# Causal mask copied into PSUM by ScalarE, a written-out table of PSUM banks, and one reciprocal moved, in a causal attention + gated feed-forward kernel

## The chip, the cores and the metric

One core of a Trainium2 chip runs the whole program once. The metric is device time in microseconds (us), the median over separate executions. Nothing is shared with other cores.

## The reference

Four sequences of 1024 tokens with 128 features go through one transformer layer with post-norm: causal attention with 8 heads of 128 and rotary positions, a residual and a layer norm, then a gated feed-forward part of width 512 with four layers, a residual and a layer norm. Cut to what matters here (all fp32):

```python
q, k, v = (jnp.einsum('btm,mhd->bthd', x, w) for w in (w_aq, w_ak, w_av))   # (4, 1024, 8, 128)
q, k = _rope(q), _rope(k)
s = jnp.einsum('bihd,bjhd->bhij', q, k) / 128
mask = (i < j)[None, None, :, :]                 # i query, j key
s = s - 1e30 * mask
p = jax.nn.softmax(s, axis=-1)
r = jnp.einsum('bhij,bjhd,hdm->bim', p, v, w_ao)
x = layernorm(x + r); x = layernorm(x + ffn(x))
```

## The kernel before

The work is 32 heads in all (8 of each of 4 sequences), one after the other, and then the feed-forward part, which the change doesn't touch. A head has 1024 queries in 8 blocks of 128, numbered `ib` 0 to 7. Block `ib` needs the keys of blocks 0 to `ib`, so its row of scores is (`ib` + 1) x 128 columns wide.

Every product that must keep fp32 accuracy is made of three fp32r matmuls (high x high, high x low, low x high), so whatever TensorE produces in PSUM is later split: ScalarE copies the high part out, VectorE subtracts it and writes the low part. One block goes through these operations:

- TensorE: `scores`. Three matmuls for each half of the row (one half up to 512 columns, two equal halves above), and one more, `ident_r` x `mask_r`, which adds -1e30 above the diagonal of the last 128 columns (L407 to L411).
- VectorE: `negative_max` (L678).
- ScalarE: `exponentiate` (L557), which writes `probs` and the row sum.
- VectorE: `inverse_sum` (L684), a reciprocal of one column.
- GpSimd: `normalize` (L802), which multiplies `probs` by it.
- TensorE: `transpose_probs` (L420), one or two fills of a PSUM bank.
- ScalarE: `transposed_high` (L569), and VectorE: `transposed_low` (L694), which write `pT`.
- TensorE: `attend` (L330 with `pT,vals`), in pieces.

The order is written out by hand as eight steps of each head, `s` = 0 to 7, and each engine runs its own part of a step in order, held only by semaphores. In step `s` TensorE issues the scores of block `s + 2` and the transposes of block `s`; VectorE issues the reciprocal of block `s + 1`, the maximum of block `s + 2` and the low halves of block `s`; ScalarE the exponential of block `s + 1` and the high halves of block `s`; GpSimd normalizes block `s + 1`. So blocks 0 and 1 of the next head already start in steps 6 and 7. Between these lies the projection of the next head's queries and keys, in four tiles of 512 columns: TensorE makes tiles 0 and 1 in step 0 and tiles 2 and 3 in step 2 (`QK_STEP`), VectorE multiplies each by sine and cosine (`rope_products`, L706 and L708), a transfer swaps halves, GpSimd adds (L813), ScalarE and GpSimd split (L579, L819). Heads go in pairs, `off` 0 and 1, here called the even and the odd head. The values for both are projected in steps 4 to 7 of the even one only (`V_STEP`, L586 on ScalarE, L726 on VectorE). A Fori loop runs over the pairs of one sequence.

PSUM has 8 banks of 512 columns. Bank 7 holds the output of `attend`. Scores of even blocks use banks 0 and 1, of odd blocks banks 2 and 3, and rows up to 512 wide leave banks 1 and 3 free for a while. Transposes (`t`), projected tiles (`qk`) and values (`v`) use banks 4, 5 and 6, and banks 1 and 3 in the steps `LEND1` and `LEND3`. `plan_banks` gives each use the bank that was used longest ago. TensorE waits, before each use, for the last reader of the bank's previous use (`wait_for_banks`): VectorE's low half for a `t` or `v`, the cosine product for a `qk` tile, the exponential for scores.

Of the kernel before, what the change touches and what calls it, by code (L numbers as in the profile page):

```python
# [27 lines left out]
P = 128  # L28
# [31 lines left out]
LEND1 = (6, 7, 0)  # L60
LEND3 = (1, 2)
FILLS_OF = [1 if i < 4 else 2 for i in range(NI)]
FIRST_FILL = [sum(FILLS_OF[:i]) for i in range(NI)]
NT = sum(FILLS_OF)
NQK, NV = len(QK_STEP), len(V_STEP)
PV_BANK = 7


def plan_banks():

    uses = {}
    last = dict.fromkeys(range(PV_BANK), 0)

    for off in range(2):
        for s in range(NI):
            ib, tile_off = (s + 2) % NI, off + (s + 2) // NI
            first = 2 * (ib % 2)
            lent = [bank for bank, free in ((1, LEND1), (3, LEND3)) if s in free]  # L80

            after = ([("t", off, FIRST_FILL[s] + k) for k in range(FILLS_OF[s])]
                     + [("qk", off + 1, j) for j in range(NQK) if QK_STEP[j] == s]
                     + [("v", 0, c) for c in range(NV) if V_STEP[c] == NI * off + s])
            for use in [("s", tile_off, ib)] + after:
                if use[0] == "s":
                    uses[use] = [first, first + 1] if ib >= 4 else [first]
                else:
                    uses[use] = [min([4, 5, 6] + lent, key=lambda b: last[b])]
                for bank in uses[use]:  # L90
                    last[bank] = len(uses)
    return uses
# [23 lines left out]
def run(nc, outer, sem, rT, ident, qk_split, v_split, xT, w_q, w_k, w_vT, w_o, rope_in, ident_in, mask_in,  # L116
# [7 lines left out]
    ident_r = sb("ident_r", [P, P], F32R, outer)  # L124
    mask_r = sb("mask_r", [P, P], F32R, outer)
# [15 lines left out]
    mask_f = sb("mask_f", [P, P], F32, pre)  # L141
# [17 lines left out]
    score_ps = psum[:, :4 * BANK].rearrange("p (s h c) -> p s h c", s=2, h=2)  # L159
# [18 lines left out]
    masks_ready = sem("masks_ready")  # L178
    W_SAVED = 16 * (len(weight_parts) + 2)


    scores_ready = (sem("scores_ready"), NI)
# [24 lines left out]
    def score_halves(ib):  # L207

        width = (ib + 1) * P
        return (1, width) if width <= BANK else (2, width // 2)  # L210
# [115 lines left out]
    def split_products(out_ap, left, right, first, last):  # L326

        terms = ((0, 0), (0, 1), (1, 0))
        for i, (a, b) in enumerate(terms):
            ins = nc.tensor.matmul(out_ap, left[a], right[b], start=first and i == 0, stop=last and i == 2)  # L330
        return ins

    with nc.Block() as block:
        @block.sync
        def _(sp):
# [5 lines left out]
            sp.dma_start(mask_f[:], mask_in).then_inc(masks_loaded, 16)  # L341
# [52 lines left out]
        def _(pe):  # L394
            def scores(head, ib):

                wait_for(pe, rope_low, head, 1 if ib < 4 else 3)

                pair, off = head if ("s", head[1], ib) in USES else (head[0] - 1, head[1] + 2)
                wait_for_banks(pe, pair, "s", off, ib)  # L400
                q, k = ([qk[:, parity(head), which, part] for part in range(2)] for which in range(2))
                halves, half = score_halves(ib)
                for h in range(halves):
                    dst = score_ps[:, ib % 2, h, :half]
                    left = [a[:, ib * P:(ib + 1) * P] for a in q]
                    right = [a[:, h * half:(h + 1) * half] for a in k]
                    nc.tensor.matmul(dst, left[0], right[0], start=True, stop=False)  # L407
                    if h == halves - 1:
                        nc.tensor.matmul(dst[:, half - P:], ident_r[:], mask_r[:], start=False, stop=False)
                    nc.tensor.matmul(dst, left[0], right[1], start=False, stop=False)  # L410
                    last = nc.tensor.matmul(dst, left[1], right[0], start=False, stop=True)  # L411
                last.then_inc(scores_ready[0], 1)

            def transpose_probs(head, ib):
                wait_for(pe, probs_ready, head, ib)
                for f in range(FILLS_OF[ib]):
                    nth = FIRST_FILL[ib] + f
                    wait_for_banks(pe, head[0], "t", head[1], nth)
                    for jb in range(4 * f, min(4 * f + 4, ib + 1)):
                        last = nc.tensor.transpose(bank("t", head[1], nth)[:, (jb % 4) * P:(jb % 4 + 1) * P],  # L420
                                                   probs[:, ib % 4, jb * P:(jb + 1) * P], ident[:])
                    last.then_inc(t_filled[0], 1)
# [49 lines left out]
            def step(head, s, b):  # L472
# [7 lines left out]
                if before_first(head) and s == NI - 2:  # L480
                    pe.wait_ge(masks_ready, 1)
# [27 lines left out]
        def _(act):  # L509
# [39 lines left out]
            def exponentiate(head, ib):  # L549

                n = parity(head) * NI + ib
                wait_for(act, max_ready, head, ib)
                old_head, old = earlier(head, ib, 4, NI)
                wait_for(act, t_filled, old_head, FIRST_FILL[old] + FILLS_OF[old] - 1)
                width = (ib + 1) * P
                halves, half = score_halves(ib)
                nc.scalar.activation(probs[:, ib % 4, :width].rearrange("p (h c) -> p h c", h=halves),  # L557
                                     score_ps[:, ib % 2, :halves, :half], ACT.Exp,
                                     bias=neg_max[:, n:n + 1], accum_out=row_sum[:, n:n + 1]).then_inc(exp_done[0], 1)

# [28 lines left out]
            def step(head, s, b):  # L589
# [3 lines left out]
                if before_first(head) and s == 1:  # L593
                    act.wait_ge(masks_loaded, 32)
                    nc.scalar.activation(ident_r[:], ident[:], ACT.Copy)
                    nc.scalar.activation(mask_r[:], mask_f[:], ACT.Copy).then_inc(masks_ready, 1)
                if before_first(head) and s == 2:
                    high_of_weights(1)
                if before_first(head) and s == 4:
                    act.wait_ge(vo_ready, 1)  # L600
# [28 lines left out]
        def _(dve):  # L629
# [44 lines left out]
            def negative_max(head, ib):  # L674
                n = parity(head) * NI + ib
                wait_for(dve, scores_ready, head, ib)
                halves, half = score_halves(ib)
                nc.vector.tensor_reduce(neg_max[:, n:n + 1], score_ps[:, ib % 2, :halves, :half], AX.XY, ALU.max,  # L678
# [65 lines left out]
            def step(head, s, b):  # L744
# [5 lines left out]
                if exists(step_on(head, (s + 1) // NI)):  # L750
# [26 lines left out]
                for target, j in rope_tasks(head, s, QK_STEP):  # L777
                    rope_products(target, j)
                if before_first(head) and s == 2:
# [14 lines left out]
        def _(pool):  # L794
            nc.gpsimd.memset(warm[:], 0.0).then_inc(warm_zero, 1)
# [605 lines left out]
```

## Time and profile before

| | |
|---|---|
| median of 3 executions | 1031.66 us (1029.73 to 1032.62) |
| the profiled execution: its time | 1031.09 us |
| its span, first to last instruction | 1029.2 us |
| TensorE, share of the span busy | 96% |
| VectorE | 79% |
| ScalarE | 58% |
| GpSimd | 53% |
| mean granted TensorE clock | 0.991 of full |

The span is 1.9 us shorter than the time. Attention fills it to about 760 us, the feed-forward part the rest. The busy shares are means over both parts, and a TensorE matmul counts as busy to its modelled end, which lies past the start of the next one, so short waits of TensorE do not show as idle. Two consecutive heads take about 46 us.

### The profile page before, as it was taken

The numbers are of one execution on the slowest core, as the hardware profiler recorded it, in microseconds if no ns is written. First come the engines' busy times: TensorE is split into PE (matmuls) and PEld (weight loads), VectorE is DVE, ScalarE is ACT, GpSimd is POOL, SyncE is SP. The second block draws the span as 40 slices with busy tenths as digits, with TensorE's granted clock in tenths as the row PEclk, the third lists the DMA queues.
The fourth block names the chain that finished last, engine by engine and source line by source line (L and its number), as shares of the span: only waits on it lengthen the run. The fifth ranks groups of instructions, "written<-read, shape, count | busy, mean of one in ns | idle before, by whom it ended". The sixth has DMA issues, their size and how long they took to land.

```text
span 1029.2 us, 19670 instructions
## 1 busy us (share of the span) xinstructions
PE 985.7 (96%) x5648; PEld 856.6 (83%) x5648; DVE 816.9 (79%) x1789; ACT 593.6 (58%) x1270; POOL 543.4 (53%) x549
## 2 busy tenths in 40 slices
PE   4899999999999999999999999999989999999995
PEld 3788898888888898888888888888878888888884
DVE  5788888888888888888888888888866778586744
ACT  3566666676656666666666666665665252433521
POOL 3666767678666767877666767766772101000000
PEclk9999999999999999999999999999999999999998
DMA  6723232222222322222235322222400000000000
GB/s 198 245 53 76 58 77 66 61 52 62 63 66 67 69 74 51 63 52 62 63 70 178 78 62 53 62 53 64 119 1 1 1 1 21 1 20 0 1 20 21
DMA packets 33979, 61.96 MB, mean 60 GB/s; under 512 B 5504, under 2 KB 7296, under 8 KB 33536
## 3 DMA queue, kind: packets, MB, share of 16 engines
q1 hardware_dynamic: 30816, 55.21, 21.5%
q10 hardware_dynamic: 3104, 6.03, 1.7%
q8 instruction: 29, 0.48, 0.2%
q14 instruction: 30, 0.25, 0.1%
HBM read 22.16 MB, written 5.24 MB: 27 GB/s over the span
## 4 chain that ended last, share of the span: by engine, by line
PE 71%; DVE 11%; issue 7%; ACT 4%; POOL 3%; DVEq 1%; ACTq 0%; POOLq 0%
PE psum L330 24%; PE psum L1047 17%; PE psum L420 9%; PE psum L410 5%; PE psum L407 5%; PE psum L1020 4%; PE psum L411 4%; DVE neg_max L678 3%; POOL probs L802 2%; DVE pT L694 2%; PE psum L1062 2%; ACT probs L557 2%; ACT pT L569 2%; DVE by_sin L706 2%; DVE by_cos L708 1%
## 5 line engine op out<-in xcount | busy, mean ns | idle before, releaser
L802 POOL TENSOR_SCALAR probs<-probs,inv_sum 128x128 f32<-128x128 f32 (+7 forms) x256 | 191.3, 747 | 222.0 <-DVE inv_sum L684 221.5
L569 ACT ACTIVATE pT<-psum 128x512 fp32r<-128x512 f32 (+3 forms) x384 | 174.2, 490 | 132.3 <-PE psum L420 130.3
L330 PE MATMUL psum<-pT,vals 128*128 128x512 f32 (+3 forms) x1152 | 243.0, 351 | 1.0 <-DVE pT L694 1.0
L557 ACT ACTIVATE probs<-psum,neg_max 128x128 f32<-128x128 f32 (+7 forms) x256 | 190.3, 743 | 85.9 <-DVE neg_max L678 80.8
L694 DVE TENSOR_TENSOR pT<-psum,pT 128x512 fp32r<-128x512 f32 (+3 forms) x384 | 201.0, 551 | 33.4 <-ACT pT L569 29.5
L678 DVE TENSOR_REDUCE neg_max<-psum 128x1 f32<-128x128 f32 (+7 forms) x256 | 191.7, 749 | 27.0 <-PE psum L411 26.1
L330 PEld LDWEIGHTS psum<-pT,vals 128*128 128x128 f32 x1152 | 188.7, 190 | 23.5 <-DVE pT L694 1.2
L420 PE MATMUL psum<-ident,probs 128*128 128x128 f32 x1152 | 173.0, 277 | 10.7 <-POOL probs L802 8.2
L1047 PE MATMUL psum<-hid,w 128*128 128x512 f32 x768 | 176.3, 390 | 0.0
L813 POOL TENSOR_TENSOR swapped<-by_cos,swapped 128x512 f32<-128x512 f32 x127 | 163.0, 1294 | 18.4 <-DMA swapped<-by_sin 17.5
L1047 PEld LDWEIGHTS psum<-hid,w 128*128 128x128 f32 x768 | 143.7, 188 | 29.5
L420 PEld LDWEIGHTS psum<-ident,probs 128*128 128x128 f32 x1152 | 134.8, 141 | 36.1 <-issue 8.6
L819 POOL TENSOR_TENSOR qk<-swapped,qk 128x512 fp32r<-128x512 f32 x126 | 162.6, 1290 | 0.0
L407 PE MATMUL psum<-qk 128*128 128x384 f32 (+5 forms) x384 | 137.7, 359 | 9.4 <-DVE qk L721 3.7
L410 PE MATMUL psum<-qk 128*128 128x384 f32 (+5 forms) x384 | 143.0, 372 | 0.0
L411 PE MATMUL psum<-qk 128*128 128x384 f32 (+5 forms) x384 | 131.6, 343 | 0.0
L330 PE MATMUL psum<-x_moving,w_stage 128*128 128x512 f32 (+1 forms) x384 | 108.1, 419 | 11.2 <-DVEq L650 8.8
L579 ACT ACTIVATE qk<-swapped 128x512 fp32r<-128x512 f32 x128 | 80.7, 631 | 41.8 <-POOL swapped L813 39.8
L1147 ACT ACTIVATE value<-psum,scales 128x512 f32<-128x512 f32 x64 | 43.0, 689 | 93.0 <-PE psum L1047 93.0
L330 PEld LDWEIGHTS psum<-x_moving,w_stage 128*128 128x128 f32 x384 | 69.7, 195 | 26.6 <-DVEq L650 8.8
L407 PEld LDWEIGHTS psum<-qk 128*128 128x128 f32 x384 | 72.8, 190 | 21.5 <-issue 10.1
L706 DVE TENSOR_TENSOR by_sin<-psum,rope 128x512 f32<-128x512 f32 x128 | 87.2, 681 | 2.5 <-DMA rope<-rope_in 2.5
(87 smaller groups left out, 1132.6 us busy)
## 6 DMA issues: line engine op xcount, KB each, us to landing
swapped<-by_sin SPq DMA_DIRECT2D x256, 128.0 KB, 2.3
w_stage<-qk_split SPq DMA_DIRECT2D x30, 256.0 KB, 2.7
wv_stage<-v_split SPq DMA_DIRECT2D x15, 256.0 KB, 2.6
ffn_raw<-g SPq DMA_DIRECT2D x2, 1024.0 KB, 7.8
out<-y SPq DMA_DIRECT2D x8, 256.0 KB, 2.0
qk_split<-rT ACTq DMA_DIRECT2D x1, 1536.0 KB, 7.7
ffn_raw<-xT SPq DMA_DIRECT2D x3, 512.0 KB, 7.8
y<-x_tok SPq DMA_DIRECT2D x1, 1536.0 KB, 8.5
```

Of the source, the lines that this page charges most:

```text
L330: ins = nc.tensor.matmul(out_ap, left[a], right[b], start=first and i == 0, stop=last and i == 2)
L407: nc.tensor.matmul(dst, left[0], right[0], start=True, stop=False)
L410: nc.tensor.matmul(dst, left[0], right[1], start=False, stop=False)
L411: last = nc.tensor.matmul(dst, left[1], right[0], start=False, stop=True)
L420: last = nc.tensor.transpose(bank("t", head[1], nth)[:, (jb % 4) * P:(jb % 4 + 1) * P], probs[:, ib % 4, jb * P:(jb + 1) * P], ident[:])
L557: nc.scalar.activation(probs[:, ib % 4, :width].rearrange("p (h c) -> p h c", h=halves), score_ps[:, ib % 2, :halves, :half], ACT.Exp, bia ...
L569: nc.scalar.activation(pT[chunk][:, 0, 4 * f:4 * f + n_blocks, (ib % 4) * P:(ib % 4 + 1) * P], bank("t", head[1], nth)[:, :n_blocks * P].r ...
L678: nc.vector.tensor_reduce(neg_max[:, n:n + 1], score_ps[:, ib % 2, :halves, :half], AX.XY, ALU.max, negate=True).then_inc(max_ready[0], 1)
L694: nc.vector.tensor_tensor(low, bank("t", head[1], nth)[:, :n_blocks * P].rearrange("p (j i) -> p j i", i=P), high.bitcast(F32), ALU.subtra ...
L802: nc.gpsimd.tensor_scalar(p, p, inv_sum[:, n:n + 1], 1.0, ALU.mult, ALU.mult).then_inc(probs_ready[0], 1)
L813: nc.gpsimd.tensor_tensor(swapped[:, j], by_cos[:, j], swapped[:, j], ALU.add).then_inc(rope_done[0], 1)
L1047: last = nc.tensor.matmul(ps[:, c, o], self.w_at(base, a, k * HID, o * P), hid[:, c, layer, b, k], start=k == 0 and i == 0, stop=k == HT - ...
```

## The change

Three edits.

1. The mask. The identity matmul goes away. A tile `mask` of 512 columns in SBUF holds zeros and, in the last 128, the triangle of -1e30. ScalarE copies as many of its last columns as needed into PSUM ahead of the scores (`write_mask`), and the three score matmuls of that piece then accumulate onto it. A row above 512 columns is now cut so that the piece with the diagonal (`near`: 256, 256, 384 and 512 columns for blocks 4 to 7) lies in the first of the two banks and the older keys in the second; the row is contiguous across both, with the key blocks rotated, and `prob_block` takes this back at the transposes. The total of columns is the same as before. ScalarE issues the mask of block `s + 3` in step `s`, right after the exponential of block `s + 1`, and waits for that exponential, which reads the same bank. TensorE issues the older keys first, then waits for the mask. At the start GpSimd writes the zeros and TensorE runs one matmul of 512 columns into banks 0 and 2.
2. The banks of `t`, `qk` and `v` come from a table over the pair of heads.
3. VectorE takes the reciprocal of block 2 in step 0, between the products of rotation tiles 0 and 1, where it stood at the start of step 1.

```diff
+MASK_COLS = BANK
+def score_layout(ib):
+    width = (ib + 1) * P
+    return width, width if ib < 4 else max(2 * P, width - BANK)
+FILL_BANKS = ((4, 6, 3, 5, 5, 6, 5, 6, 1, 5, 3, 4), (6, 3, 4, 4, 6, 4, 5, 6, 4, 1, 6, 3))
+QK_BANKS = ((1, 5, 5, 4), (5, 4, 5, 6))
+V_BANKS = (4, 4, 6, 1)
...
+    def score_row(ib):
+        width, near = score_layout(ib)
+        first = BANK - near if ib >= 4 else 0
+        return score_ps[:, ib % 2, first:first + width]
+    def masked_piece(ib):
+        return score_row(ib)[:, :score_layout(ib)[1]]
...
-                halves, half = score_halves(ib)
-                for h in range(halves):
-                    dst = score_ps[:, ib % 2, h, :half]
-                    left = [a[:, ib * P:(ib + 1) * P] for a in q]
-                    right = [a[:, h * half:(h + 1) * half] for a in k]
-                    nc.tensor.matmul(dst, left[0], right[0], start=True, stop=False)
-                    if h == halves - 1:
-                        nc.tensor.matmul(dst[:, half - P:], ident_r[:], mask_r[:], start=False, stop=False)
-                    nc.tensor.matmul(dst, left[0], right[1], start=False, stop=False)
-                    last = nc.tensor.matmul(dst, left[1], right[0], start=False, stop=True)
+                left = [a[:, ib * P:(ib + 1) * P] for a in q]
+                width, near = score_layout(ib)
+                if width > near:
+                    split_products(score_row(ib)[:, near:], left, [a[:, :width - near] for a in k], True, True)
+                wait_for(pe, mask_written, head, ib)
+                last = split_products(masked_piece(ib), left, [a[:, width - near:width] for a in k], False, True,
+                                      onto_mask=True)
...
+            def write_mask(head, ib):
+                wait_for(act, exp_done, *earlier(head, ib, 2, NI))
+                near = score_layout(ib)[1]
+                nc.scalar.activation(masked_piece(ib), mask[:, MASK_COLS - near:], ACT.Copy).then_inc(mask_written[0], 1)
...
                 if exists(ahead):
                     exponentiate(ahead, (s + 1) % NI)
+                if exists(step_on(head, (s + 3) // NI)):
+                    write_mask(step_on(head, (s + 3) // NI), (s + 3) % NI)
...
-                if exists(step_on(head, (s + 1) // NI)):
+                if exists(step_on(head, (s + 1) // NI)) and s != 1:
                     inverse_sum(step_on(head, (s + 1) // NI), (s + 1) % NI)
...
                 for target, j in rope_tasks(head, s, QK_STEP):
+                    if s == 0 and j == 1 and exists(head):
+                        inverse_sum(head, 2)
                     rope_products(target, j)
```

On ScalarE, step 5 of the first (even) head: exponential, rotated tile, two high halves of the transposed block, values. Before:

```order
L557 ACTIVATE probs,row_sum<-psum,neg_max 128x896 [waits t_filled,max_ready]
L579 ACTIVATE qk<-swapped 128x512 [waits rope_done]
L569 ACTIVATE pT<-psum 128x4x128 [waits t_filled]
L569 ACTIVATE pT<-psum 128x2x128 [waits t_filled]
L586 ACTIVATE vals<-psum 128x512 [waits v_projected]
L557 ACTIVATE probs,row_sum<-psum,neg_max 128x1024 [waits t_filled,max_ready]
L579 ACTIVATE qk<-swapped 128x512 [waits rope_done]
```

The same step with the change (line numbers are those of the changed kernel):

```order
L573 ACTIVATE probs,row_sum<-psum,neg_max 128x896 [waits t_filled,max_ready]
L580 ACTIVATE psum<-mask 128x128 [waits exp_done]
L600 ACTIVATE qk<-swapped 128x512 [waits rope_done]
L590 ACTIVATE pT<-psum 128x4x128 [waits t_filled]
L590 ACTIVATE pT<-psum 128x2x128 [waits t_filled]
L607 ACTIVATE vals<-psum 128x512 [waits v_projected]
L573 ACTIVATE probs,row_sum<-psum,neg_max 128x1024 [waits t_filled,max_ready]
L580 ACTIVATE psum<-mask 128x256 [waits exp_done]
```

A copy into PSUM now stands behind every exponential, and everything else of the step moves down behind it.

On VectorE, step 0 of the same head and the beginning of step 1: products of tiles 0 and 1, then the reciprocal and the maximum. Before:

```order
L706 TENSOR_TENSOR by_sin<-psum,rope 128x512 [waits rope_low,swap_done0,qk_projected]
L708 TENSOR_TENSOR by_cos<-psum,rope 128x512
L706 TENSOR_TENSOR by_sin<-psum,rope 128x512 [waits rope_low,swap_done1,qk_projected]
L708 TENSOR_TENSOR by_cos<-psum,rope 128x512
L661 TENSOR_TENSOR rT<-raw_w,rT 128x6x128 [waits qk_w_high]
L684 RECIPROCAL inv_sum<-row_sum 128x1 [waits exp_done]
L678 TENSOR_REDUCE neg_max<-psum 128x1 [waits scores_ready]
```

With the change:

```order
L728 TENSOR_TENSOR by_sin<-psum,rope 128x512 [waits rope_low,swap_done0,qk_projected]
L730 TENSOR_TENSOR by_cos<-psum,rope 128x512
L706 RECIPROCAL inv_sum<-row_sum 128x1 [waits exp_done]
L728 TENSOR_TENSOR by_sin<-psum,rope 128x512 [waits rope_low,swap_done1,qk_projected]
L730 TENSOR_TENSOR by_cos<-psum,rope 128x512
L684 TENSOR_TENSOR rT<-raw_w,rT 128x6x128 [waits qk_w_high]
L700 TENSOR_REDUCE neg_max<-psum 128x1 [waits scores_ready]
```

The reciprocal moves ahead of two products, which now stand behind its wait for the exponential. (The row on `rT` is a single one of the first head.)

On TensorE, the scores of block 6, before:

```order
L407 MATMUL psum<-qk 128x448 [waits exp_done,rope_low]
L410 MATMUL psum<-qk 128x448
L411 MATMUL psum<-qk 128x448
L407 MATMUL psum<-qk 128x448
L409 MATMUL psum<-mask_r,ident_r 128x128
L410 MATMUL psum<-qk 128x448
L411 MATMUL psum<-qk 128x448
```

With the change:

```order
L346 MATMUL psum<-qk 128x512 [waits exp_done,rope_low]
L346 MATMUL psum<-qk 128x512 x2
L346 MATMUL psum<-qk 128x384 [waits mask_written]
L346 MATMUL psum<-qk 128x384 x2
```

One matmul is gone, and the second piece has a wait of its own.

## Rows read from the trace of the kernel before

**Rows 1.** The page's part 1: busy time of each engine, share, instructions.

```profile
PE 985.7 (96%) x5648; PEld 856.6 (83%) x5648; DVE 816.9 (79%) x1789; ACT 593.6 (58%) x1270; POOL 543.4 (53%) x549
```

**Rows 2.** Windows: start:end, length, busy us (instructions) by engine, PEclk, DMA share, GB/s.

```profile
454.30:466.60 12.30, 12.30 (x89) 11.44 (x88) 10.96 (x23) 10.44 (x25) 9.05 (x9) 1.00 0.10 28
478.40:488.60 10.20, 9.84 (x65) 8.54 (x64) 8.40 (x18) 8.15 (x20) 8.97 (x9) 1.00 0.00 0
466.60:478.40 11.80, 11.68 (x66) 10.04 (x65) 10.01 (x21) 5.54 (x13) 7.00 (x8) 1.00 0.50 114
```

**Rows 3.** Timeline of TensorE, block 7's scores, even head: start, us, instruction.

```profile
455.56 0.40 PE L407 MATMUL psum<-qk 128*128 128x512 f32 x1
...
456.26 0.39 PE L407 MATMUL psum<-qk 128*128 128x512 f32 x1
...
457.06 0.82 PE L420 MATMUL psum<-ident,probs 128*128 128x128 f32 x6
```

**Rows 4.** Groups by shape, ScalarE's copies: busy us, mean ns, idle before.

```profile
L569 ACT ACTIVATE pT<-psum 128x512 fp32r<-128x512 f32 x192 | 111.0, 596 | 84.3 <-PE psum L420 82.6
L579 ACT ACTIVATE qk<-swapped 128x512 fp32r<-128x512 f32 x128 | 80.7, 631 | 41.8 <-POOL swapped L813 39.8 <-DVE swapped L715 0.2
...
L569 ACT ACTIVATE pT<-psum 128x384 fp32r<-128x384 f32 x64 | 31.5, 492 | 5.9 <-PE psum L420 5.5
...
L569 ACT ACTIVATE pT<-psum 128x256 fp32r<-128x256 f32 x64 | 24.8, 387 | 34.8 <-PE psum L420 34.8
...
L569 ACT ACTIVATE pT<-psum 128x128 fp32r<-128x128 f32 x64 | 17.7, 276 | 7.4 <-PE psum L420 7.3
```

**Rows 5.** Timeline of ScalarE, steps 4 to 7 of an even head.

```profile
454.94 0.77 ACT L569 ACTIVATE pT<-psum 128x512 fp32r<-128x512 f32 x2 [2.13 <-PE psum L420]
...
457.15 0.20 ACT L557 ACTIVATION_READ_ACCUMULATOR probs<-psum,neg_max 128x1 f32 x1
457.24 0.63 ACT L579 ACTIVATE qk<-swapped 128x512 fp32r<-128x512 f32 x1
...
459.11 1.11 ACT L557 ACTIVATE probs<-psum,neg_max 128x1024 f32<-128x1024 f32 x1
...
462.83 1.09 ACT L569 ACTIVATE pT<-psum 128x512 fp32r<-128x512 f32 x2 [0.29 <-PE psum L420]
```

**Rows 6.** The chain that ended last, even into odd head: start, us, what.

```profile
464.06 0.68 DVE pT L694
...
468.67 0.61 DVE by_cos L708
469.28 0.04 issue
469.32 0.41 PE psum L407
```

**Rows 7.** Timeline of TensorE: block 2's transposes of that odd head.

```profile
470.42 0.49 PE L420 MATMUL psum<-ident,probs 128*128 128x128 f32 x3
```

**Rows 8.** The chain that ended last, steps 5 to 7 of the odd head.

```profile
480.91 1.24 DVE neg_max L678
...
483.81 1.11 POOL probs L802
484.91 0.12 issue
485.03 0.67 PE psum L420 x4
```

**Rows 9.** Timeline of ScalarE, odd into even head.

```profile
485.72 1.09 ACT L569 ACTIVATE pT<-psum 128x512 fp32r<-128x512 f32 x2 [0.39 <-PE psum L420]
486.69 0.48 ACT L557 ACTIVATE probs<-psum,neg_max 128x256 f32<-128x256 f32 x1
```

**Rows 10.** Timeline of TensorE: block 3's scores of the next head.

```profile
488.60 0.40 PE L407 MATMUL psum<-qk 128*128 128x512 f32 x1
```

**Rows 11.** The chain that ended last, steps 0 to 2 of an even head.

```profile
444.08 0.68 DVE by_sin L706
...
445.36 0.07 DVE inv_sum L684
```

**Rows 12.** Timeline of GpSimd, the same place: block 2 normalized.

```profile
445.63 0.59 POOL L802 TENSOR_SCALAR probs<-probs,inv_sum 128x384 f32<-128x384 f32 x1 [3.23 <-DVE inv_sum L684]
```

**Rows 13.** Timeline of TensorE, the same place: block 2 transposed.

```profile
446.35 0.43 PE L420 MATMUL psum<-ident,probs 128*128 128x128 f32 x2 [0.19 <-DVE pT L694]
```

More of the change, by code:

```diff
@@ L79, in plan_banks @@
             first = 2 * (ib % 2)
[L80 to L91, printed above, removed]
+            uses["s", tile_off, ib] = [first, first + 1] if ib >= 4 else [first]
+            for nth in range(FIRST_FILL[s], FIRST_FILL[s] + FILLS_OF[s]):
+                uses["t", off, nth] = [FILL_BANKS[off][nth]]
+            for j in range(NQK):
+                if QK_STEP[j] == s:
+                    uses["qk", off + 1, j] = [QK_BANKS[off][j]]
+            for c in range(NV):
+                if V_STEP[c] == NI * off + s:
+                    uses["v", 0, c] = [V_BANKS[c]]
     return uses
@@ L122, in sb @@
         return where.enter_context(nc.sbuf_tensor(name, shape, dt))
[L124 to L125 removed]
+    mask = sb("mask", [P, MASK_COLS], F32, outer)
     ffn = FeedForward(nc, outer, sem, rT, ident, ffn_raw, ffn_loaded, x_tok, scales_in, out)
@@ L324, in wait_for_banks, with split_products @@
                 break
-    def split_products(out_ap, left, right, first, last):
+    def split_products(out_ap, left, right, first, last, onto_mask=False):
         terms = ((0, 0), (0, 1), (1, 0))
         for i, (a, b) in enumerate(terms):
-            ins = nc.tensor.matmul(out_ap, left[a], right[b], start=first and i == 0, stop=last and i == 2)
+            ins = nc.tensor.matmul(out_ap, left[a], right[b], start=first and i == 0, stop=last and i == 2,
+                                   skip_group_check=onto_mask)
         return ins
@@ L479, in step @@
                     last.then_inc(vo_ready, 1)
-                if before_first(head) and s == NI - 2:
-                    pe.wait_ge(masks_ready, 1)
+                    pe.wait_ge(mask_zero, 1)
+                    pe.wait_ge(masks_loaded, 32)
+                    for masked_bank in (0, 2):
+                        nc.tensor.matmul(psum[:, masked_bank * BANK:(masked_bank + 1) * BANK], mask[:, :P], mask[:],
+                                         start=True, stop=True).then_inc(scores_opened, 1)
                 if is_first(head) and s == 1:
@@ L676, in negative_max @@
                 wait_for(dve, scores_ready, head, ib)
-                halves, half = score_halves(ib)
-                nc.vector.tensor_reduce(neg_max[:, n:n + 1], score_ps[:, ib % 2, :halves, :half], AX.XY, ALU.max,
+                nc.vector.tensor_reduce(neg_max[:, n:n + 1], score_row(ib), AX.X, ALU.max,
                                         negate=True).then_inc(max_ready[0], 1)
@@ L777, in step @@
                 for target, j in rope_tasks(head, s, QK_STEP):
+                    if s == 0 and j == 1 and exists(head):
+                        inverse_sum(head, 2)
                     rope_products(target, j)
+                if s == 0 and exists(head) and not rope_tasks(head, s, QK_STEP):
+                    inverse_sum(head, 2)
                 if before_first(head) and s == 2:
@@ L794, in _ @@
         def _(pool):
+            nc.gpsimd.memset(mask[:, :MASK_COLS - P], 0.0).then_inc(mask_zero, 1)
             nc.gpsimd.memset(warm[:], 0.0).then_inc(warm_zero, 1)
```

29 lines of the change are left out of this document (13 added, 16 removed).

## The prediction, made before the changed kernel ran

> **What bounds the kernel now.** I read the shares first. TensorE is busy 96% of the span [rows 1], which says that a removed matmul should shorten the time by its own length. But a busy matmul is counted past the start of the next, so I read the windows and then the chain that ended last through a pair of heads. ScalarE is busy 10.44 of 12.30 us in steps 4 to 7 of the even head, 8.15 of 10.20 in those of the odd one, and only 5.54 of 11.80 in between [rows 2]. It has room on average and hardly any where the even head projects the values. The chain then shows that TensorE is only one of three bounds in turn:
>
> - In steps 2 to 4 of each head TensorE itself is the chain.
> - In steps 4 to 7 of the even head it runs through ScalarE, which works from 454.94 with a single gap of 0.29 us ahead of 462.83 [rows 5]. It goes on through VectorE: low halves of block 7 at 464.06, and the cosine product of tile 1, which ends at 469.28. That product frees the bank in which the odd head's block 4 gets its scores, and TensorE starts them at 469.32 [rows 6].
> - In the odd head it goes maximum of block 7 (480.91, 1.24 us), exponential, reciprocal, normalization (483.81, 1.11 us), transposes at 485.03 [rows 8]. No TensorE work is in it for 4 us.
> - At the start of the even head it goes rotation products, reciprocal of block 2 at 445.36 [rows 11], normalization at 445.63 after GpSimd sat idle for 3.23 us [rows 12], and so to the transposes of block 2 at 446.35, ahead of which TensorE was idle 0.19 us [rows 13].
>
> **The mask matmuls removed.** Block 7 shows the same three matmuls with and without the mask. The first half takes 455.56 to 456.26, 0.70 us; the second, with it, 456.26 to 457.06, 0.80 us [rows 3]. A mask matmul costs 0.10 us of TensorE's time. There are 8 x 32 = 256 of them: 26 us if TensorE were the bound everywhere. The new cut of the rows has the same columns in all, so it costs nothing by itself.
>
> **The mask copies added.** No row shows ScalarE copying from SBUF into PSUM. The nearest rows are its copies from PSUM: 276, 387, 492 and 596 ns for 128, 256, 384 and 512 columns; from SBUF to SBUF 512 columns take 631 ns [rows 4]. I take the first set, since they have all four sizes, and 0.04 us more for the wait on its own exponential, which is what a released engine took at 469.28 [rows 6]. Without a wait the next instruction starts 0.11 us ahead of the end of the row-sum read (457.24 against 457.15 + 0.20) [rows 5]; this overlap is lost ahead of the copy and comes back behind it. So the prices are 0.32, 0.43, 0.53 and 0.64 us. Per head there are one, three, two and two of these sizes: 3.95 us. Two heads' 7.9 us of ScalarE against some 18 us idle in 46 us fit on average. Bounds for one copy: 0.1 us less (a faster write to PSUM, or the wait hidden) and 0.15 us more (the slower SBUF source, and a late wake-up).
>
> The Trainium skill (ScalarE: Activation LUTs, "Step-by-step: what each stage is for") says that ScalarE writes into PSUM faster than into SBUF. All rows 4 write into SBUF, so the trace can't say. If the rule takes 0.1 us off each copy, the sum below ends near 1009.
>
> **What each stretch of a pair gains**, taken at TensorE's own positions:
>
> (a) Step 4 of the even head to block 2's transposes of the odd one. The copy for block 7 lies in the 2.13 us in which ScalarE is idle ahead of 454.94 [rows 5] and costs nothing. Those for blocks 0, 1 and 2 stand in the full stretch: 0.32 + 0.43 + 0.53 = 1.28, less the gap of 0.29, so block 7's high halves come 1.0 us later. VectorE waits for them and is full from 464.06 on. Queued behind are values, block 2's maximum and the rotation products, all 1.0 us later, and 0.1 more for the reciprocal now ahead of tile 1: its cosine product ends at 470.4 and not at 469.28 [rows 6]. By the table, block 4's scores no longer wait for it, since bank 1 now held value tile 3; block 2's transposes do (bank 4), and they stand at 470.42 today [rows 7]. The table takes back just what the copies cost. Gain 0.
>
> (b) From there to step 4 of the odd head, TensorE bound: two masks, 0.2.
>
> (c) Odd head to block 7's transposes. Between the exponentials of blocks 6 and 7 stands the copy for block 0 (0.32), which makes ScalarE, and not the maximum, the last to be ready. The 0.2 of (b) is taken back, and 485.03 [rows 8] stays. Gain -0.2.
>
> (d) To block 2's transposes of the next even head. The copies for blocks 1 and 2 cost 0.96 less the gap of 0.39, so block 1's exponential starts at 487.3 and not at 486.69 [rows 9]; with 0.57 for itself and 0.64 for block 3's copy this ends at 488.5. Block 3's scores start at 488.60 today [rows 10]: just held. Behind them two masks (0.2) and the 0.19 us wait for the reciprocal [rows 13] go, which now comes after tile 0, some 1.2 us earlier (tile 1's products start at 444.08, the reciprocal stood at 445.36) [rows 11]. Gain 0.4.
>
> (e) To step 4 of that head: two masks, 0.2.
>
> Sum 0 + 0.2 - 0.2 + 0.4 + 0.2 = 0.6 us a pair, 16 pairs: 10 us. What the start gains and loses (two opening matmuls, a memset, while TensorE still waits) is left out. The moved bank waits around tiles 0 and 1 give perhaps 1 us more. The profiled execution took 1031.1 us with its 1.9 us outside the span; less 11 this is 1020. The median of the runs is 0.6 us above that execution, within their spread.
>
> **The rivals.**
>
> - *ScalarE's copies are hidden.* If the copies are 0.1 cheaper, or the chain gives way because the table and the early reciprocal free more than I see, TensorE sets the pace again: 26 us of masks, and 16 x 2 x 0.19 = 6 of waits for block 2, so 1000. For it: ScalarE is idle over a third of attention. Against it: the 0.29 gap [rows 5]. With only the cheaper copies, 7 of them stand on the chain of a pair (three in (a), four in (c) and (d)): 7 x 0.1 x 16 = 11 us, 1009.
> - *Slower: the copies stretch the exponential-to-transposes chain.* Each copy stands ahead of the high halves and of the next exponential. With 7 copies on the chain, 0.6 / 7 = 0.09 us more per copy takes all the gain; 0.15 more gives 7 x 0.15 x 16 = 17 us: 1037. The place is block 7's transposes in both heads. For it: there is no slack there. Against: everything measured near is copied at the price that I took.
> - *No change*: 0.05 to 0.12 us more per copy, between the two, 1028 to 1034.
> - *It doesn't do what it says*: TensorE's 0.10 us for a mask may be hidden by weight loads, so that only the waits change. Rows 3 speak against it; it would give the slower case.
>
> **The numbers.** Part of the gain returned, 1010 to 1028: 0.50. Hidden (998 to 1010): 0.25. No change: 0.12. Slower: 0.13. The likeliest gives 1020. The range of 1003 to 1032 leaves out about 2 in 10. A measurement of this kernel tells 0.3% (3 us) from no change: faster 0.76, same 0.12, slower 0.12.
>
> **What would show it.** Right: ScalarE's busy share up by some 110 us; its copies at 0.28 to 0.60 us; windows of steps 4 to 7 of the even head as long as today (12.3 us) with ScalarE nearly full; the gain in steps 0 to 4; GpSimd's 3.2 us wait ahead of block 2 down to about 2; maxima and exponentials of the same length as now. Wrong: TensorE waiting for the mask itself in many steps, exponentials of blocks 0 and 7 more than 1 us later against TensorE, or reads of rows across two banks that got longer.

## The result and the profile after

| | before | changed |
|---|---|---|
| median | 1031.25 us (1029.45 to 1032.62, 5 runs) | 1014.91 us (1014.57 to 1015.58, 5 runs) |
| the profiled execution: time, span | 1031.09 us, 1029.2 us | 1014.79 us, 1012.9 us |

The ratio is 0.9844, with a 95% interval of 0.9832 to 0.9857: 16.3 us less, where 11 were forecast. The granted clock is the same (0.990 of full, 0.991 before).

Shares of the page, part 1, which answers to [rows 1], and part 4, the chain that ended last by engine (before, the same line of the page had TensorE 71%, VectorE 11%, ScalarE 4%, GpSimd 3%):

```profile
PE 968.7 (96%) x5396; PEld 828.6 (82%) x5396; DVE 815.9 (81%) x1789; ACT 694.5 (69%) x1524; POOL 543.7 (54%) x550
PE 59%; ACT 11%; POOL 10%; DVE 9%; issue 7%; DMA 2%; DVEq 0%; ACTq 0%; POOLq 0%; SPq 0%
```

ScalarE is busy 100.9 us more (694.5 - 593.6), and it is now a larger part of the chain. TensorE is still "96% busy": the share hides the whole change.

The groups by shape: ScalarE's new copies (L580), and one group that answers to [rows 4]. Columns: busy us, mean ns of one | idle before:

```profile
L590 ACT ACTIVATE pT<-psum 128x512 fp32r<-128x512 f32 x192 | 108.9, 584 | 22.5 <-PE psum L434 22.5
...
L580 ACT ACTIVATE psum<-mask 128x512 f32<-128x512 f32 x64 | 38.5, 602 | 2.0
L580 ACT ACTIVATE psum<-mask 128x256 f32<-128x256 f32 x96 | 37.3, 388 | 3.0
L580 ACT ACTIVATE psum<-mask 128x384 f32<-128x384 f32 x64 | 31.7, 496 | 2.0
...
L580 ACT ACTIVATE psum<-mask 128x128 f32<-128x128 f32 x32 | 9.0, 282 | 1.0
```

A copy takes what one from PSUM takes, and the wait ahead of it adds 8.0 us of idle time over 256 copies, 0.03 each. ScalarE's idle time ahead of `transposed_high` of 512 columns fell from 84.3 us [rows 4] to 22.5: the copies fill it.

To see where the time came from I take the prediction's own five stretches of a pair: each begins and ends at the start of the transposes of some block, rows of L434 in TensorE's timeline. Here is one pair; `x5` are block 4's transposes, `x3` block 2's, `x8` block 7's:

```profile
445.30 0.71 PE L434 MATMUL psum<-ident,probs 128*128 128x128 f32 x5
...
461.02 0.55 PE L434 MATMUL psum<-ident,probs 128*128 128x128 f32 x3
...
468.79 0.71 PE L434 MATMUL psum<-ident,probs 128*128 128x128 f32 x5
...
475.58 1.09 PE L434 MATMUL psum<-ident,probs 128*128 128x128 f32 x8 [0.48 <-POOL probs L829]
...
482.35 0.49 PE L434 MATMUL psum<-ident,probs 128*128 128x128 f32 x3
...
490.06 0.71 PE L434 MATMUL psum<-ident,probs 128*128 128x128 f32 x5
```

The differences are (a) 15.72, (b) 7.77, (c) 6.79, (d) 6.77 and (e) 7.71 us. The same differences as means over the 12 pairs in the middle of the span, from the one traced execution of each kernel (the experiments come below):

| us | (a) | (b) | (c) | (d) | (e) | pair |
|---|---|---|---|---|---|---|
| before | 16.01 | 7.93 | 6.65 | 7.29 | 7.97 | 45.86 |
| changed | 15.81 | 7.75 | 6.78 | 6.75 | 7.75 | 44.84 |
| gain | 0.20 | 0.18 | -0.13 | 0.54 | 0.22 | 1.02 |
| forecast | 0 | 0.2 | -0.2 | 0.4 | 0.2 | 0.6 |
| mask alone | 16.73 | 7.70 | 6.78 | 7.59 | 7.75 | 46.55 |
| table alone | 15.83 | 7.97 | 6.65 | 7.29 | 7.98 | 45.73 |
| reciprocal alone | 16.08 | 7.94 | 6.65 | 6.97 | 7.94 | 45.58 |
| table and reciprocal | 15.78 | 7.94 | 6.65 | 6.75 | 7.94 | 45.06 |
| before, no mask matmuls | 15.79 | 7.75 | 6.65 | 7.29 | 7.79 | 45.27 |
| changed, no copies | 15.42 | 7.71 | 6.65 | 6.54 | 7.75 | 44.06 |
| changed, dearer copies | 16.52 | 7.75 | 7.16 | 7.23 | 7.95 | 46.61 |
| copies for 4 to 7 only | 16.02 | 7.71 | 6.65 | 6.79 | 7.70 | 44.87 |
| copies for 4 to 6 only | 15.71 | 7.71 | 6.65 | 6.66 | 7.72 | 44.45 |

16 pairs x 1.02 = 16.3 us: the pairs hold the gain. (The changed kernel begins its first pair 2.5 us later than before, and that pair is 3.4 us shorter and not 1.0; the two about cancel.)

The chain that ended last, in stretch (a) of the pair above (start, us, what), answers to [rows 5, 6]:

```profile
453.38 0.48 ACT vals L607
453.86 0.36 ACT probs L573 x2
...
454.68 0.59 ACT pT L590
...
455.90 0.68 DVE pT L716
...
460.37 0.61 DVE by_cos L730
461.02 0.55 PE psum L434 x3
```

This is what the prediction said: the chain runs through ScalarE and VectorE to tile 1's cosine product, and what waits for that is now block 2's transposes, not block 4's scores. In the 12 pairs the transposes start 0.08 us after that product ends; before it was 1.17, with block 4's scores between.

The windows of the changed kernel answer to [rows 2] (same columns; steps 4 to 7 of the even head, what follows, steps 4 to 7 of the odd one from the start of its block 4's transposes at 468.79, all cut to the same lengths as before; the second overlaps the third by 0.6 us):

```profile
445.30:457.60 12.30, 12.24 (x86) 11.05 (x85) 10.58 (x22) 11.46 (x28) 9.68 (x10) 1.00 0.13 42
457.60:469.40 11.80, 11.71 (x67) 10.13 (x66) 10.92 (x23) 7.65 (x17) 7.03 (x8) 1.00 0.49 112
468.79:478.99 10.20, 9.66 (x61) 8.06 (x60) 8.25 (x19) 9.37 (x23) 9.65 (x10) 1.00 0.05 17
```

ScalarE's busy time, the fourth of the five, is 11.46 of 12.30 us (10.44 before), 7.65 (5.54) and 9.37 of 10.20 (8.15). The copies nearly filled ScalarE in both crowded stretches.

One wait of TensorE for a mask is not in the idle notes. It stands at the end of the odd head, where block 2's scores of the next head follow block 7's transposes. First two rows of TensorE before; then, in the changed kernel, ScalarE's mask copy for block 2 and the scores that accumulate onto it:

```profile
485.03 1.09 PE L420 MATMUL psum<-ident,probs 128*128 128x128 f32 x8 [0.23 <-POOL probs L802]
485.88 0.42 PE L407 MATMUL psum<-qk 128*128 128x384 f32 x1
...
476.14 0.49 ACT L580 ACTIVATE psum<-mask 128x384 f32<-128x384 f32 x1
476.69 0.79 PE L346 MATMUL psum<-qk 128*128 128x384 f32 x3
```

Before, the scores start 0.85 us after the transposes (485.88 - 485.03). Now it is 1.11 (476.69 - 475.58), 0.06 after the copy's end at 476.63. In the 12 pairs these scores start 0.05 us after the copy's end in nine and 0.14 after it in three. The transposes count as busy to their modelled end, so this wait shows as no idle time.

### The profile page after: what moved, and what is told of

The parts are those of the page before. It is cut to its first block, busy times and chain, and to the rows that moved or that the text cites. A ratio compares the mean times of both kernels' runs of the same rounds, so it can differ in the third digit from the quotient of the medians.

```text
span 1012.9 us, 19514 instructions
## 1 busy us (share of the span) xinstructions
PE 968.7 (96%) x5396; PEld 828.6 (82%) x5396; DVE 815.9 (81%) x1789; ACT 694.5 (69%) x1524; POOL 543.7 (54%) x550
## 4 chain that ended last, share of the span: by engine, by line
PE 59%; ACT 11%; POOL 10%; DVE 9%; issue 7%; DMA 2%; DVEq 0%; ACTq 0%; POOLq 0%; SPq 0%
PE psum L346 28%; PE psum L1074 17%; PE psum L434 6%; ACT probs L573 5%; PE psum L1047 4%; ACT pT L590 4%; POOL probs L829 4%; DVE by_cos L730 3%; POOL qk L846 3%; POOL swapped L840 3%; PE psum L1089 2%; DVE by_sin L728 2%; DVE pT L716 1%; DVE neg_max L700 1%; DMA rope<-rope_in 1%
## 5 line engine op out<-in xcount | busy, mean ns | idle before, releaser
L346 PE MATMUL psum<-qk 128*128 128x512 f32 (+3 forms) x1152 | 254.7, 348 | 7.2 <-ACT psum L580 3.4
L346 PEld LDWEIGHTS psum<-qk 128*128 128x128 f32 x1152 | 195.4, 190 | 37.5 <-issue 9.1
L434 PE MATMUL psum<-ident,probs 128*128 128x128 f32 x1152 | 175.6, 277 | 14.3 <-POOL probs L829 11.6
L590 ACT ACTIVATE pT<-psum 128x512 fp32r<-128x512 f32 (+3 forms) x384 | 170.7, 479 | 25.1 <-PE psum L434 24.4
L434 PEld LDWEIGHTS psum<-ident,probs 128*128 128x128 f32 x1152 | 132.4, 141 | 41.2 <-issue 13.4
L580 ACT ACTIVATE psum<-mask 128x256 f32<-128x256 f32 (+3 forms) x256 | 116.6, 455 | 8.0
L730 DVE TENSOR_TENSOR by_cos<-psum,rope 128x512 f32<-128x512 f32 x128 | 86.9, 679 | 0.0
```

Of the source, the lines that this page charges most:

```text
L580: nc.scalar.activation(masked_piece(ib), mask[:, MASK_COLS - near:], ACT.Copy).then_inc(mask_written[0], 1)
L590: nc.scalar.activation(pT[chunk][:, 0, 4 * f:4 * f + n_blocks, (ib % 4) * P:(ib % 4 + 1) * P], bank("t", head[1], nth)[:, :n_blocks * P].r ...
L730: nc.vector.tensor_tensor(by_cos[:, j], projected, rope[:, 0, c * BANK:(c + 1) * BANK], ALU.mult).then_inc(cos_done[0], 1)
```

## The experiments

Each was timed against the kernel before on its own chip (medians there 1031.1 to 1031.4 us).

### The two halves of the change: mask only, and all but the mask

`e1_mask_only` has the mask copies, with the old planner of banks and the old place of the reciprocal. `e2_table_recip` is the kernel before with the other two edits. It leaves `scores` with its mask matmul as it was; the planner takes the banks from the table, and on VectorE (cut with `...`):

```diff
-                if exists(step_on(head, (s + 1) // NI)):
+                if exists(step_on(head, (s + 1) // NI)) and s != 1:
                     inverse_sum(step_on(head, (s + 1) // NI), (s + 1) % NI)
...
                 for target, j in rope_tasks(head, s, QK_STEP):
+                    if s == 0 and j == 1 and exists(head):
+                        inverse_sum(head, 2)
                     rope_products(target, j)
+                if s == 0 and exists(head) and not rope_tasks(head, s, QK_STEP):
+                    inverse_sum(head, 2)
```

> The kernel before with the mask copies alone: banks still from the old plan, block 2's reciprocal still at the start of step 1. Theory 1 (TensorE, ScalarE and VectorE set the pace in turn; the table and the early reciprocal cut the chain where the copies lengthen it): the 1.0 us of the three copies in the even head now reaches block 4's scores of the odd head through the cosine product of tile 1, and block 2's transposes wait for the late reciprocal. Two masks fewer in each of two stretches give 0.4 us back, so about +0.5 us a pair: 1035 to 1045, slower than before. Theory 2 (TensorE's own length decides, the copies are hidden, and the other two edits are decoration): 1015, like the full change.

> The kernel before with the bank table and the early reciprocal, mask matmuls kept, no copies. Theory 1: the waits ahead of block 4's scores in the odd head and of block 2's transposes in the even one go, 0.2 to 0.4 us a pair, 3 to 6 us: 1025 to 1028. Theory 2: 1031, no change, since no TensorE work goes.

Measured: mask only 1041.82 us (ratio 1.0109, 1.0094 to 1.0125), 10.5 us *slower* than before. All but the mask 1018.61 us (0.9883, 0.9867 to 0.9898), 12.7 us faster. The first was expected; the second gained two to four times what I had for it. So the two small edits carry the change, and the mask edit loses alone and gains 3.7 us (1018.61 - 1014.91) on top of them.

The chain of mask only, the same place as above:

```profile
467.70 0.59 ACT pT L594
...
468.93 0.68 DVE pT L720
...
473.35 0.61 DVE by_cos L734
473.96 0.04 issue
474.00 1.16 PE psum L350 x6
475.16 0.33 PE psum L438 x3
```

Under the old planner the scores of block 4 (L350) wait for the cosine product, as in [rows 6], and 1.16 us of them stand between it and block 2's transposes. In the changed kernel the transposes follow it at once. Stretch (a) is 16.73 us in one and 15.81 in the other.

### Each of the two small edits alone

> The kernel before with the bank table alone. With the table and the early reciprocal together the time was 1018.6. Theory 1a: the table is the larger part, since today a cosine product holds block 4's scores of the odd head and a low half of block 7 holds tile 0 of the even one; the reciprocal then becomes what block 2's transposes wait for: 1022 to 1026. Theory 1b: the two cut the same chain, which runs through the rotation products, so that one alone gives next to nothing: 1029 to 1031.

> The kernel before with the early reciprocal alone. Theory 1a: it frees block 2's transposes in the even head, by the 0.19 to 0.3 us that TensorE stands there, while in the odd head the cosine product still holds the scores ahead of them: 3 to 5 us less, 1026 to 1028. Theory 1b: nothing without the table, 1031.

Measured: table alone 1028.12 us (0.9975, 0.9965 to 0.9985), reciprocal alone 1028.11 us (0.9970, 0.9960 to 0.9980). 3 us each, 6 together, but the two in one kernel give 12.7. The table's time lies between the ranges of its two theories, so neither was right; the reciprocal came out at the edge of its range. (By the table of stretches the two bring 0.13 and 0.28 us a pair alone, 0.80 together: 2, 4.5 and 12.8 us. The traced execution with the reciprocal alone, 1025.15 us, is the fastest of its nine, so its row is the least sure.) TensorE's timeline in stretch (d) shows where the rest of the 12.7 comes from. First the kernel before, transposes of blocks 0, 1 and 2 (`x1`, `x2`, `x3`):

```profile
486.64 0.33 PE L420 MATMUL psum<-ident,probs 128*128 128x128 f32 x1
...
489.41 0.38 PE L420 MATMUL psum<-ident,probs 128*128 128x128 f32 x2
...
492.34 0.54 PE L420 MATMUL psum<-ident,probs 128*128 128x128 f32 x3 [0.18 <-DVE pT L694]
```

The table alone:

```profile
484.83 0.32 PE L416 MATMUL psum<-ident,probs 128*128 128x128 f32 x1
...
487.45 0.38 PE L416 MATMUL psum<-ident,probs 128*128 128x128 f32 x2
...
490.53 0.55 PE L416 MATMUL psum<-ident,probs 128*128 128x128 f32 x3 [0.33 <-DVE pT L690]
```

The reciprocal alone:

```profile
482.70 0.33 PE L420 MATMUL psum<-ident,probs 128*128 128x128 f32 x1
...
485.46 0.38 PE L420 MATMUL psum<-ident,probs 128*128 128x128 f32 x2
...
488.06 0.49 PE L420 MATMUL psum<-ident,probs 128*128 128x128 f32 x3
```

Both together:

```profile
478.04 0.33 PE L416 MATMUL psum<-ident,probs 128*128 128x128 f32 x1
...
480.65 0.38 PE L416 MATMUL psum<-ident,probs 128*128 128x128 f32 x2
...
483.26 0.49 PE L416 MATMUL psum<-ident,probs 128*128 128x128 f32 x3
```

From block 0 to 1 and from 1 to 2: before 2.77 and 2.93 us, table 2.62 and 3.08, reciprocal 2.76 and 2.60, both 2.61 and 2.61. The table takes a wait out of the first part, and TensorE then stands 0.15 us longer ahead of block 2, since that is held by the reciprocal, a point on another engine that did not move: it stands 4.62 us after block 0's transposes in both kernels (means of 12 pairs), and 3.42 after them once it is moved. The idle note grows from 0.18 to 0.33. The reciprocal alone takes out the second wait. Only together do both go, 0.48 us.

The notes name VectorE's low half (`DVE pT`), not the normalization that needs the reciprocal. Here are GpSimd's normalization of block 2 with the table alone, and the low half with the reciprocal alone:

```profile
489.81 0.58 POOL L798 TENSOR_SCALAR probs<-probs,inv_sum 128x384 f32<-128x384 f32 x1 [3.23 <-DVE inv_sum L680]
487.99 0.41 DVE L694 TENSOR_TENSOR pT<-psum,pT 128x256 fp32r<-128x256 f32 x1
```

With the table alone the normalization ends at 490.39, 0.14 us ahead of the transposes. With the reciprocal alone the low half ends at 488.40, 0.34 us *after* the transposes have started at 488.06, so they don't wait for it. The wait is for the normalization, and in two kernels the low half merely ends at the same moment.

The kernel before without its mask matmuls (below) says the same: stretch (d) stays at 7.29, since what TensorE saves on masks it loses again ahead of block 2.

In stretch (a) the table gains 0.18, the reciprocal alone costs 0.07, and both gain 0.23. The cost is the reciprocal's own place in VectorE's queue, ahead of tile 1's products: the cosine product, which the old banks make block 4's scores wait for, ends 0.06 us later (14.91 against 14.85 us after block 4's transposes). With the table alone, block 2's transposes of the odd head start 0.13 us after their normalization ends, so there too the late reciprocal holds back part of what the table frees.

### No mask at all, in the old and in the new kernel

In these two the triangle is left unmasked. `e3_no_mask_matmul` is the kernel before without the 256 identity matmuls; `e4_no_copies` is the changed kernel without copies and waits:

```diff
-                wait_for(pe, mask_written, head, ib)
-                last = split_products(masked_piece(ib), left, [a[:, width - near:width] for a in k], False, True, onto_mask=True)
+                last = split_products(masked_piece(ib), left, [a[:, width - near:width] for a in k], True, True)
...
-                if exists(step_on(head, (s + 3) // NI)):
-                    write_mask(step_on(head, (s + 3) // NI), (s + 3) % NI)
```

> The kernel before without its 256 mask matmuls and nothing in their place; the triangle above the diagonal of each last block isn't masked. Theory 1: they are worth their 0.10 us only in the stretches in which TensorE is the chain, about 0.6 us a pair: 10 us less, 1019 to 1024. Theory 2: all 256 count, 26 us less: 1005.

> The changed kernel (table, early reciprocal, new cut of the rows, no mask matmul) without the mask copies and the waits on them; the triangle isn't masked. It shows what the copies cost in the changed kernel. Theory 1: they cost 1.0 us in the even head and some 0.5 in the odd one, until TensorE becomes the bound (1.6 us of masks and 0.4 us of waits a pair less than before, 32 us at most): 1000 to 1006. Theory 2: the copies are hidden, so 1015, like the full change.

Measured: 1022.48 us (0.9918, 0.9904 to 0.9931) and 1003.40 us (0.9732, 0.9719 to 0.9746). Both lie in the ranges of the first theory. The 256 matmuls are worth 8.8 us in the old order of waits (1031.31 - 1022.48) and 15.2 in the new (1018.61 - 1003.40), of 26 at 0.10 each. (The 15.2 holds the new cut of the rows too. In (b) and (e), where TensorE is the bound, the two kernels without masks differ by 0.04 us each, so the cut is worth little there.) The copies cost 11.5 us in the new one. 15.2 - 11.5 = 3.7 is what the mask edit brings. By the table of stretches the copies cost 0.39 in (a), 0.13 in (c) and 0.21 in (d), and in (b) and (e), which TensorE bounds, some 0.05 together. In (d) all of it lies between the transposes of blocks 7 and 0, where TensorE waits for the mask of block 2 (1.81 us, for 1.60 without copies). This also answers the hidden rival: the copies are not hidden, since leaving them out gains 11.5 us. Only without them does the time, 1003, come near that rival's 1000.

### Dearer copies

Each mask copy gets a copy of one column and a wait for it ahead of itself:

```diff
+                nc.scalar.activation(spare[:], spare[:], ACT.Copy).then_inc(spare_done[0], 1)
+                wait_for(act, spare_done, head, ib)
                 nc.scalar.activation(masked_piece(ib), mask[:, MASK_COLS - near:], ACT.Copy).then_inc(mask_written[0], 1)
```

> The changed kernel with a one-column copy, and a wait for it, ahead of every mask copy on ScalarE: some 0.24 us more for each. It tests how many copies of a pair stand on the chain. Theory 1: seven (blocks 0 to 2 in the even head, 0 to 3 in the odd one): 7 x 0.24 x 16 = 27 us more, 1042, or somewhat less since the first part of it is taken from gaps: 1032 to 1042. Theory 2 (hidden): 1015 to 1018.

Measured: 1042.56 us (1.0116, 1.0100 to 1.0131), 27.7 more than the changed kernel. The added row of the groups:

```profile
L582 ACT ACTIVATE spare<-spare 128x1 f32<-128x1 f32 x256 | 52.0, 203 | 8.0
```

203 ns and two waits of 0.03 us, of which one was there: about 0.24 us. With 7 copies of a pair on the chain, 7 x 0.24 x 16 = 27, as measured. By stretch, the pair grows by 0.71 us in (a), 0.38 in (c), 0.48 in (d) and 0.20 in (e). Three copies of 0.24 fit (a). The four of the odd head would be 0.96 in (c) and (d), where 0.86 stand, and (e) was to have none. So the count of seven holds as a sum, and place by place only in (a). It holds for dearer copies alone: leaving all of them out gains 11.5 us, where seven full prices, less the two gaps of the prediction, would be (3.20 - 0.68) x 16 = 40.

### Copies only where ScalarE has room

`e7_copies_4_to_7` keeps copies for blocks 4 to 7 and gives blocks 0 to 3 an identity matmul again, in plain fp32:

```diff
+                if ib < 4:
+                    nc.tensor.matmul(dst, left[0], right[0], start=True, stop=False)
+                    nc.tensor.matmul(dst[:, near - P:], ident[:], mask[:, MASK_COLS - P:], start=False, stop=False)
```

> The changed kernel with mask copies for blocks 4 to 7 alone. Blocks 0 to 3 get their mask by a matmul of identity and triangle again (plain fp32, 128 columns), their rows right-aligned in the bank; no opening matmuls. The copies for blocks 0 to 3 stand in steps 5 to 7 and 0, where ScalarE is full and the chain runs through it; those for 4 to 7 in steps 1 to 4, where it is idle for some us and TensorE is the chain. Theory 1 (turns): the masks of blocks 4 to 7 are still saved where TensorE is the chain, and the 11.5 us that the copies cost go down to a few: 1007 to 1012, faster than the changed kernel. Theory 2 (ScalarE's total load counts, or the 128 matmuls that come back count in full, 13 us): 1015 to 1025.

Measured: 1015.76 us (0.9854, 0.9841 to 0.9868), no better than the changed kernel. The first theory missed; the second, that the matmuls put back count in full, had 1015 to 1025. Its chain, block 2's scores:

```profile
455.08 0.23 PE psum L425
455.30 0.22 PE psum L426 x2
455.52 0.18 PE psum L427
455.70 0.17 PE psum L428
```

The mask matmul (L426) in fp32 is two instructions and 0.22 us, not 0.10. That is 0.12 x 4 x 32 = 15 us more of TensorE's time, in a kernel whose chain here is TensorE all through (from 445 to 466 us of the span). So I took the mask in fp32r, as the kernel before has it, and copies for blocks 4, 5 and 6 (`e9`) or 5 and 6 (`e10`). (Some small tensors of the second norm were placed elsewhere to make room.)

```diff
+COPIED = (4, 5, 6)
...
+                if ib not in COPIED:
+                    nc.tensor.matmul(dst, left[0], right[0], start=True, stop=False)
+                    nc.tensor.matmul(dst[:, near - P:], ident_r[:], mask_r[:], start=False, stop=False)
```

> Table and early reciprocal; mask copies for blocks 4, 5 and 6 alone, and for the other five blocks the fp32r mask matmul of the kernel before (one instruction of 0.10 us, where the plain fp32 one of the run before was two). The second norm's small tensors move into space that attention doesn't use. Theory 1 (turns): against table and reciprocal alone (1018.6) six mask matmuls a pair go from stretches in which TensorE is the chain, and no copy stands where ScalarE is full: 6 x 0.1 x 16 = 10 us, 1007 to 1010, faster than the changed kernel. Theory 2 (where the copies stand doesn't matter, the saving is by count): the changed kernel gained 3.7 us over table and reciprocal with eight blocks, so three blocks give 1.4: 1017.

> The same with copies for blocks 5 and 6 alone. Theory 1: 4 x 0.1 x 16 = 6.4 us less than table and reciprocal alone, 1011 to 1013. Theory 2: 1018.

Measured: 1007.64 us (0.9770, 0.9757 to 0.9784) and 1010.60 us (0.9796, 0.9783 to 0.9809). The first was expected; the second is 0.4 us below its range. The first is 7.3 us below the changed kernel and is the best of all that masks. Its page, parts 1 and 4:

```profile
PE 969.4 (96%) x5552; PEld 844.6 (84%) x5552; DVE 814.6 (81%) x1789; ACT 629.7 (63%) x1366; POOL 543.8 (54%) x550
PE 83%; DVE 5%; issue 4%; POOL 3%; ACT 3%; DMA 1%; ACTq 0%; SPq 0%; POOLq 0%; DVEq 0%
```

TensorE has 0.7 us more to do than in the changed kernel, ScalarE 65 us less, and the chain is TensorE to 83%. The copies for blocks 4 to 6 are issued in steps 1 to 3, where ScalarE idles. In the stretches, (a), (c) and (d) fall to 15.71, 6.65 and 6.66, and (b) and (e) keep what the changed kernel had.

## Why the prediction was nearly right

The time came out 5.1 us under the forecast of 1020 and inside the range, and the mechanism held: three engines bound the pair in turn, and what a copy costs or a matmul gives depends on where it stands. The total is nearer than its parts, and that was luck. The table and the reciprocal were expected at 3 to 6 us (in `e2`) and brought 12.7. That left 5 to 8 of the 11 us to the mask edit on top of them, which brought 3.7. The two misses go opposite ways.

- **Mask matmuls, 0.10 us each where TensorE bounds.** Right. (b) and (e) gained 0.18 and 0.22, for 0.2 and 0.2.
- **Price of a copy, 0.32 to 0.64 us with its wait.** Right: 282 to 602 ns and 0.03 idle. Writing into PSUM from SBUF (602 ns) takes as long as reading PSUM (584) and hardly less than SBUF to SBUF (624 in the same trace, into fp32r), so the case of copies 0.1 us cheaper fell. The rule of the Trainium skill (ScalarE: Activation LUTs, "Step-by-step: what each stage is for") that ScalarE writes into PSUM faster than into SBUF holds here by 22 ns in 512 columns, no more.
- **(a), gain 0.** Mis-sized; 0.20 measured. Forecast was that block 7's high halves come 1.0 us later against block 4's transposes, and the cosine product's end 1.1. In the pair shown, the high halves start 454.68 - 445.30 = 9.38 us after them, which before was 462.83 [rows 5] - 454.31 = 8.52: 0.86. (454.31 is the start of block 4's transposes in the trace of before.) The mean of the 12 pairs is 0.86 too, and the product ends 0.88 us later in them (15.73 against 14.85), with 0.06 of that from the reciprocal. So VectorE was as full as forecast, and the term that was too large is the 1.0 us for the copies. (In the single pair shown the product moves by 0.71 only, 15.68 against 14.97 in [rows 6], a pair above the mean of before.)
- **(c), gain -0.2.** Right in sign, -0.13 measured. ScalarE, and not the maximum, is last in the odd head, as forecast: block 7's exponential starts 3.94 us after block 4's transposes, for 3.81 before, which is the whole loss. The 0.2 of (b) was not taken back in full.
- **(d), gain 0.4.** Mis-sized, and its parts wrongly named: 0.54 measured. I had 0.2 from two masks and 0.19 from the wait [rows 13]. The runs show 0.54 from table and reciprocal alone and nothing more from the mask edit, since the copies cost there what the matmuls gave (0.21 each way). The step that failed is "the 0.19 us wait for the reciprocal", for two reasons. Idle time in a row is what is left of a wait after another wait ahead of it has made TensorE late: take the first away and the idle note is larger, 0.33. And the note is less than what the wait costs, since the matmul ahead is counted to its modelled end: with a note of 0.18, moving the reciprocal alone brought block 2's transposes 0.33 us nearer to block 1's (2.93 to 2.60). A second step of (d) failed as well. The copies were to be "just held", with block 3's scores as the place to watch; the place was block 2's scores, which wait for their mask and cost 0.2.
- **The moved bank waits, perhaps 1 us in all.** Too small. The table alone brings 3 us, and with it the reciprocal brings 9.5 (1028.12 - 1018.61) and not 3.
- **No change, 1028 to 1034.** By its own prices, 0.05 to 0.12 us for each of 7 copies, this rival's range is 1026 to 1033.

Of the signs named ahead: ScalarE's busy time rose by 101 us, for 110. The copies' times were right. The copies left steps 4 to 7 of the even head as full as forecast (11.46 of 12.30). GpSimd's wait ahead of block 2, 3.23 us before [rows 12], is here

```profile
481.26 0.59 POOL L829 TENSOR_SCALAR probs<-probs,inv_sum 128x384 f32<-128x384 f32 x1 [2.03 <-DVE inv_sum L706]
```

as forecast. Of the signs of being wrong, the exponentials of blocks 0 and 7 came at most 0.72 us later against block 4's transposes. The maxima and exponentials of 1024 columns take on average what they took (1.22 and 1.12 us). TensorE's idle time for the mask itself is small in the list of waits (us in all, times, longest):

```profile
PE psum L346 <- ACT psum L580: 3.4, 5, 1.4
```

But this list misses the wait for block 2's mask, once a pair, shown above.

What stays open: how the 8.1 us between `e7` and `e9` divide between the fp32 matmuls and block 7's copy. By the table of stretches 0.31 us a pair lie in (a), 0.13 in (d) and none elsewhere, 7 us in all, so the 15 us of TensorE's time did not count in full. No run makes a copy cheaper, so what that would be worth is not shown either.

## What to carry to other kernels

Where several engines are the bound in turn, price an edit at each place and not by its busy time: the same 256 matmuls were worth 8.8 us, 15.2 us or, traded for copies, a loss of 10.5. Move work to another engine only at the places where that engine idles: copying three masks of eight beat copying all by 7.3 us. A busy engine may be waiting: compare the distance between two starts before and after, not the idle time alone. A short wait in a trace may be the remainder of a longer one behind another wait; edits that remove two waits in a row have to be tried together (3 and 3 us alone, 12.7 together).

## What the hardware showed that was not expected

A plain fp32 matmul of 128 columns is recorded as two instructions and takes 0.22 us of TensorE's chain, against 0.10 for the same product in fp32r. By the starts, block 1's scores of the even head with it take 0.58 us (452.11 to 452.69), and with the fp32r mask matmul of the kernel before 0.47 (461.72 to 462.19). A ScalarE copy of a single column takes 203 ns, against 282 for 128 columns and 602 for 512.
